# A two-layer graph network on one core: one-hot picks of source rows in place of a count matrix

## What is computed

```python
def _sage_layer(x, src, dst, deg_inv, Wl, bl, Wr):
    n = x.shape[0]
    agg = jax.ops.segment_sum(x[src], dst, num_segments=n) * deg_inv
    h = agg @ Wl.T + bl + x @ Wr.T
    norm = jnp.maximum(jnp.linalg.norm(h, axis=-1, keepdims=True), EPS)
    return jax.nn.relu(h / norm)

h = _sage_layer(x, src, dst, deg_inv, Wl0, bl0, Wr0)
h = _sage_layer(h, src, dst, deg_inv, Wl1, bl1, Wr1)
x = _layernorm(x + h)
```

## Time and profile before

| | |
|---|---|
| median of three runs | 7893.84 us (7893.78 to 7914.73) |
| profiled execution, span from first to last instruction | 8201.9 us |
| of it the edge stage with set-up | up to about 5,139 us |
| segment sum of layer 0 | 5,454 to 6,680 us |
| segment sum of layer 1 | 6,763 to 8,026 us, with node stages before and behind |
| one superblock in the profile | 86.6 to 87.7 us |

### The profile page before, as it was taken

One profiled execution on the slowest core, in us unless ns is written; L12 is line 12 of the kernel. 1 busy time (PEld: TensorE's weight loads), 2 busy tenths in 40 slices (PEclk: granted clock), 3 DMA queues, 4 the chain that ended last, 5 costly groups with the idle time before them and its releaser, 6 DMA issues. The chain is left out here.

```text
span 8201.9 us, 138821 instructions
## 1 busy us (share of the span) xinstructions
PE 7072.6 (86%) x39416; PEld 5215.0 (64%) x39416; DVE 4581.6 (56%) x16310; ACT 3033.9 (37%) x6076; POOL 5844.8 (71%) x4866
## 2 busy tenths in 40 slices
PE   5898988888998889989899999878888887888883
PEld 4777777777777777877788778543333353333332
DVE  5777777777777633333333333346666656666663
ACT  2222222222222222222222222356666666666664
POOL 5888888888778888888888887336666655666663
PEclk7777777777777766676666666679999978999995
DMA  4333333333333322222222222221111111111111
GB/s 125 33 35 35 34 34 34 34 35 34 34 34 34 33 27 27 27 27 27 27 28 27 28 27 26 82 54 20 20 20 20 21 42 34 21 21 20 20 21 50
DMA packets 652915, 273.41 MB, mean 33 GB/s; under 512 B 544598, under 2 KB 600314, under 8 KB 652360
## 3 DMA queue, kind: packets, MB, share of 16 engines
q0 software_dynamic: 325280, 163.91, 19.0%
q1 hardware_dynamic: 326500, 105.06, 5.9%
q10 hardware_dynamic: 900, 1.60, 0.1%
HBM read 189.59 MB, written 80.61 MB: 33 GB/s over the span
## 5 line engine op out<-in xcount | busy, mean ns | idle before, releaser
L653 POOL DMA_INDIRECT future<-sbuf,sidx x1564 | 2495.2, 1595 | 507.1 <-issue 457.8
L639 POOL DMA_INDIRECT gbuf<-in_x_dram,gidx x1564 | 1563.3, 1000 | 482.6 <-issue 471.1
L1441 ACT CAST dense<-bank 128x512 bf16<-128x512 f32 x2744 | 1572.9, 586 | 834.3 <-PE bank L1452 514.2
L1465 PE MATMUL bank<-dense,wide 128*128 128x512 bf16 x2744 | 1066.9, 389 | 248.2 <-ACT dense L1441 125.7
L1377 DVE TENSOR_SCALAR at_dst<-iota,metaf 128x512 bf16<-128x512 f16 x2758 | 919.0, 360 | 575.0 <-PE bank L1452 425.1
L1343 POOL DMA_INDIRECT gb<-x,nidx x728 | 781.3, 1073 | 495.6 <-DVE at_dst L1377 293.6
L1452 PE MATMUL bank<-at_dst,at_src 128*128 128x512 bf16 x2744 | 1057.0, 389 | 70.2 <-DVE at_dst L1377 70.2
L1343 POOL DMA_INDIRECT gb<-h,nidx x728 | 781.1, 1073 | 467.8 <-DVE at_dst L1377 271.8
L1466 PE MATMUL bank<-dense,wide 128*128 128x512 bf16 x2744 | 1062.8, 387 | 0.0
L965 PEld LDWEIGHTS bank<-w1pe,featT 96*128 96x128 f32 x3128 | 722.3, 269 | 305.8 <-issue 305.2
L966 PE MATMUL bank<-w1px,srcT 65*128 65x128 f32 x3128 | 815.5, 354 | 0.0
(11 more groups left out here) (255 smaller groups left out, 11505.8 us busy)
## 6 DMA issues: line engine op xcount, KB each, us to landing
gbuf<-in_x_dram,gidx POOLq DMA_INDIRECT x1564
comb<-in_edge_attr_dram SPq DMA_DIRECT2D x391, 64.0 KB
future<-sbuf,sidx POOLq DMA_INDIRECT x1564
blkb<-blkrow SPq DMA_DIRECT2D x210, 98.0 KB
future<-zero POOLq DMA_DIRECT2D x16, 800.0 KB, 17.7
fut<-future SPq DMA_DIRECT2D x100, 125.0 KB
gb<-x,nidx POOLq DMA_INDIRECT x732, 2.4
gb<-h,nidx POOLq DMA_INDIRECT x732, 2.5
```

What stands on the lines that cost most here:

```text
L639: pool.indirect_dma_start(out=gbuf[:, b, q, :], out_offset=None, in_=x[:, :], in_offset=bass.IndirectOffsetOnAxis(ap=gidx[:, b, q:q + 1], ...
L653: pool.indirect_dma_start(out=future[q][:, :], out_offset=bass.IndirectOffsetOnAxis(ap=sidx[:, b, q:q + 1], axis=0), in_=sbuf[:, b, q, :], ...
L1441: act.copy(dense[:, b % AR, :], psA[b % AR][:, :]).then_inc(t_cp, 1)
L1465: pe.matmul(psHM[:, :], pieces[:, b, 0:2 * D], dense[:, b % AR, :], start=(b == 0), stop=(b == BLOCKS - 1))
```

## The change

`adjacency` goes. In its place `rows_of` (PE) multiplies `at_src` by the block's `pieces` (192 columns: three pieces of 64) and so picks for each of the 128 slots the row of its source node, still as three exact bf16 pieces. Two steps make a pair: both picks write one bank of `psA` (192 columns each), and ACT copies both at once (2x192 columns) as bf16 into `rows16`. `apply` then uses the picked rows as weights and streams `at_dst` (not `dense`): two matmuls of 512 columns a step, as before. There are two banks of `psA`, two buffers of `rows16`, and two each of `psHM` and `psL`, used by turns of the superblock; the banks of `sums` go from three to two.

For the picks `at_src` has to be the other way round: source lanes on the partitions, slots along the row. The node stage before the layers turns the lane table of each superblock by a matmul with an identity (14), ACT copies them (4 copies), and one transfer stores them as `lanes`. In the layers SP loads seven rows of it at a time, broadcast to 128 partitions (`laneb`, 3 buffers, 196 loads of 128x896 f16 a layer), and `sources` becomes one TENSOR_SCALAR comparing that with the lane number.

`at_dst` has 14 buffers instead of 7; DVE makes it 8 steps ahead and, from step 14 on, waits for `apply` of 14 steps before instead of for `adjacency`. The sum of the three 64x512 results of a superblock moves to step 4 of the next one (`add_dense`); ACT moves the middle one in the third pair of the next.

```diff
-AR = 3
+AR = 2
+LEAD = 8
+DR = 14
+PW = XPCS * 64
...
             @block.scalar
             def _(act):
+                act.wait_ge(c_turned, 1)
+                for k in range(4):
+                    n = min(4, SBS - 4 * k)
+                    act.copy(lane16[:, 4 * k:4 * k + n, :],
+                             bank[1 + k][0:BLOCKS, 0:n * P].rearrange("b (s p) -> b s p", s=n)).then_inc(c_lane, 1)
+                act.wait_ge(c_lane, 4)
+                act.dma_start(lanes.rearrange("s b p -> b s p"), lane16[:, :, :]).then_inc(c_lane_st, 16)
...
             def _(pe):
+                for i in range(SBS):
+                    last = pe.matmul(bank[1 + i // 4][0:BLOCKS, (i % 4) * P:(i % 4 + 1) * P], meta[:, i, 0, :],
+                                     ident16[:, :], start=True, stop=True)
+                last.then_inc(c_turned, 1)
                 pe.wait_ge(c_ones, 1)
+                pe.wait_ge(c_lane, 4)
...
-SUM_SLOT = [0, 1, 2] * 4 + [1]
+SUM_SLOT = [0, 1] * 6 + [0]
...
                     def sources(k):
-
-                        dve.tensor_tensor(at_src[:, k % 2, :, :], iota16[:, 0:P].unsqueeze(1).to_broadcast([P, RING, P]),
-                                          metaf[:, 0, k * RING:(k + 1) * RING].unsqueeze(2).to_broadcast([P, RING, P]),
-                                          ALU.is_equal)
+                        dve.wait_ge(t_ln[k % 3], 16 * (k // 3 + 1))
+                        if k >= 2:
+                            dve.wait_ge(t_A, RING * (k - 1))
+                        dve.tensor_scalar(at_src[:, k % 2, :, :], laneb[:, k % 3, :, :], lane1[:, 0:1], None,
+                                          ALU.is_equal).then_inc(t_src, 1)
-                    def destinations(b):
-                        dve.tensor_scalar(at_dst[:, b % RING, :], iota16[:, :], metaf[:, 1, b:b + 1], None,
+                    def destinations(t):
+                        if t >= DR:
+                            dve.wait_ge(t_ap, t - DR + 1)
+                        b = t % BLOCKS
+                        dve.tensor_scalar(at_dst[:, t % DR, :], iota16[:, :], metaf[:, b:b + 1], None,
                                           ALU.is_equal).then_inc(t_at, 1)
...
-                    for i in range(SBS):
-                        for b in range(BLOCKS):
-                            act.wait_ge(t_A, BLOCKS * i + (b + 1))
-                            act.copy(dense[:, b % AR, :], psA[b % AR][:, :]).then_inc(t_cp, 1)
+                    for j in range(STEPS // 2):
+                        act.wait_ge(t_A, 2 * j + 2)
+                        act.copy(rows16[:, j % AR, :, 0:PW],
+                                 psA[j % AR][:, 0:2 * PW].rearrange("p (h k) -> p h k", h=2)).then_inc(t_cp, 1)
...
-                    def adjacency(i, b):
-                        pe.wait_ge(t_at, BLOCKS * i + (b + 1))
-                        pe.matmul(psA[b % AR][:, :], at_src[:, (b // RING) % 2, b % RING, :], at_dst[:, b % RING, :],
-                                  start=True, stop=True).then_inc(t_A, 1)
...
+                        if t % 2 == 0 and j >= AR:
+                            pe.wait_ge(t_cp, j - AR + 1)
+                        pe.matmul(psA[j % AR][:, (t % 2) * PW:(t % 2 + 1) * PW], at_src[:, (t // RING) % 2, t % RING, :],
+                                  pieces[:, b, :], start=True, stop=True).then_inc(t_A, 1)
...
+                        pe.wait_ge(t_at, t + 1)
+                        if b == 0 and i >= 2:
+                            pe.wait_ge(t_acc, ADDS * (i - 1) + ADDS - 1)
+                            pe.wait_ge(t_ms, i)
+                        pe.matmul(psHM[i % 2][:, :], rows16[:, j % AR, t % 2, 0:2 * D], at_dst[:, t % DR, :],
+                                  start=(b == 0), stop=(b == BLOCKS - 1))
+                        pe.matmul(psL[i % 2][:, :], rows16[:, j % AR, t % 2, 2 * D:4 * D], at_dst[:, t % DR, :],
                                   start=(b == 0), stop=(b == BLOCKS - 1)).then_inc(t_ap, 1)
```

More of the change, by code:

```diff
@@ L1019, in build @@
         mostrow = tmp("mostrow", [1, 4])
+        lane16 = tmp("lane16", [BLOCKS, SBS, P], F16)
         (c_left, c_mostT) = [tsem(f"c_left{i}") for i in range(2)]
+        (c_turned, c_lane, c_lane_st) = [tsem(f"c_lane{i}") for i in range(3)]
         (c_ones, c_s1, c_s2, c_sum, c_P, c_C, c_past, c_max, c_inv, c_I, c_flow, c_F, c_fT, c_H, c_hb, c_hc, c_O, c_yc,
@@ L1314, in build @@
             t_cp = lsem("cp")
-            t_end = lsem("end")
+            t_pad = lsem("pad")
+            t_src = lsem("src")
+            t_ln = [lsem(f"ln{b}") for b in range(3)]
             t_ap = lsem("ap")
@@ L1331, in _ @@
                         sp.dma_start(xf[:, c % 3, :, :], blocks_of[:, c * XB:(c + 1) * XB, :]).then_inc(t_xf[c % 3], 16)
+                        if c < 3:
+                            load_lanes(c)
+                    for k in range(3, CHUNKED):
+                        load_lanes(k)
                 @block.gpsimd
@@ L1475, in sums @@
                         for q in range(TILES):
-                            last = pe.matmul(psG[SUM_SLOT[m]][0:D, 0:W], gb1[:, m, q, :], oneh[:, ONE_SLOT[m], q, :],
+                            last = pe.matmul(psG(SUM_SLOT[m]), gb1[:, m, q, :], oneh[:, ONE_SLOT[m], q, :],
                                              start=(q == 0), stop=(q == TILES - 1))
                         last.then_inc(t_S, 1)
-                    for i in range(SBS):
-                        for b in range(BLOCKS):
-                            adjacency(i, b)
-                            if b >= 2:
-                                apply(i, b - 2)
-                            for m in range(POOLG):
-                                if b == TAKE[m]:
-                                    sums(i, m)
-                        apply(i, BLOCKS - 2)
-                        apply(i, BLOCKS - 1)
+                    for j in range(STEPS // 2 + 1):
+                        if j < STEPS // 2:
+                            rows_of(2 * j)
+                            rows_of(2 * j + 1)
+                        if j >= 1:
+                            for t in (2 * j - 2, 2 * j - 1):
+                                apply(t)
+                                for m in range(POOLG):
+                                    if t % BLOCKS == TAKE[m]:
+                                        sums(t // BLOCKS, m)
             clear(edge_sems)
@@ L1533, in _ @@
                             for q in range(TILES):
-                                last = pe.matmul(psG[0][0:D, 0:W], gb1[:, 0, q, :], oneh[:, 0, q, :],
+                                last = pe.matmul(psG(0), gb1[:, 0, q, :], oneh[:, 0, q, :],
                                                  start=(q == 0), stop=(q == TILES - 1))
```

109 lines of the change are left out of this document (69 added, 40 removed).

## The result

| | before | changed |
|---|---|---|
| median of 13 runs each | 7897.33 us | 7937.40 us |
| lowest, highest | 7892.24, 7914.73 | 7910.74, 7947.37 |
| ratio | | 1.0043, 95% interval 1.0036 to 1.0051 |
| profiled span | 8201.9 us | 7939.0 us |

The change makes the kernel slower, by 0.43%, where 7708 us and 2.4% faster were forecast, outside of the range of 7590 to 7880.

What follows compares the result with a forecast made beforehand. PE was taken to bound the segment sums before, POOL after: 28 x (76.3 - 69.4) = 193 us, less 2.4 + 4.8, gives 186 us saved, so 7893.8 - 186 = 7708 us; range 7590 to 7880.

Steps and rivals of the forecast that it cites:

- The time of a superblock before, 76.3 us from 87.3 less the 308 us: Segment sums before: profiled 87.3 us a superblock includes 11.0 us of late matmuls absent from timed runs, leaving 76.3.
- the rival that took the lateness for real, at 7445 us: Segment sums: late matmuls also occur when timed, so 87.3 us a superblock before and 71 after; 7445 us, chance 0.08.
- Span and median do come together: Changed kernel's profile: forecast a span some 300 us over the median; both coming together would show the late matmuls real.
- PE, 59.6 us: PE in the segment sums: 49 pairs of steps, 50.5 us, plus 9.1 for gathered groups make 59.6 us a superblock.
- the hidden hand-over: PE to ACT and back: picks and copy take about 0.8 us, hidden behind 1.03 us of PE work.
- the loads of lanes: SP's 196 loads a layer: one used each 4.9 us, three in flight, so they are hidden.
- The superblock's start: Start of each superblock: PE's 1.4 us wait while DVE empties the accumulators goes away.
- POOL is the bound: Segment sums after the change: POOL needs 65.4 us or more a superblock, against PE's 59.6 and DVE's 47.
- How long its gathers are: POOL's gathers: 4.0 us a superblock left over the bare floor of 65.4, where 6.4 stood, giving 69.4 us.
- I let these two cancel: POOL's gathers away from the superblock's start: at_src shrinking by 0.7 us offsets at_dst made in runs of about four.
- The rival "slower": POOL's gathers under DVE's runs of at_src and at_dst: mean gather over 1.16 us, about 8030 us; chance 0.11.
- The Trainium skill's rule: DVE and GpSimd share SBUF ports: the new at_src blocks GpSimd's descriptor writes, up to 5.0 us a superblock, about 7850.

Runs made afterwards that it cites:

- the second trace: The kernel before, unchanged, profiled once more: 7907.0 us in one execution, profiled span 7905.1 us.

## Why the prediction was wrong, point by point

- **The time of a superblock before, 76.3 us from 87.3 less the 308 us**: right in kind and 0.5 us high; the second trace has 75.8. That choice held, and the rival that took the lateness for real, at 7445 us, fell with it. Span and median do come together in the changed kernel, which I had named as a sign for that rival; the sign was badly chosen, since they also come together in the second trace of before.
- **PE, 59.6 us**: right, 59.6 measured without the gathers; picks 0.085 us apart, a pair 1.03. Its own 74.0 before measured 74.1.
- **ACT's copy 0.48 us, the hidden hand-over, at_src 0.36 us, the loads of lanes**: right. The copy has 479 ns, the new `at_src` stands 5741.97 - 5741.61 = 0.36 us ahead of the next instruction, and without the loads nothing is won.
- **The superblock's start**: right, PE's accumulators make it wait no more.
- **POOL is the bound**: right.
- **How long its gathers are**: this step failed. I had 6.4 us over the floor, took 1.9 off for the start, and wrote of the rest "I let these two cancel" and of "runs of about four". The runs became eight. DVE's limit of 14 buffers lets it start four steps at once behind a group, and in the time of those PE, with a step each 0.52 us against DVE's 0.26, frees the next ones; 4 / (1 - 0.26 / 0.52) = 8 `at_dst`, all that there are up to the next group, where I stopped counting at the first four. The term was 4.0 us over the floor of 65.4. Measured are 11.9, 65.36 + 11.86 = 77.2 in place of 69.4, and 28 x 7.8 = 218 us are most of the miss of 229. The kernel before had 52 x (1.060 - 0.952) = 5.6.
- **The loop**: I treated DVE's time as free, because it has 47 us of work in 69. But the idle time lies in 13 lumps, each of them a wait for the slower POOL, and each is followed by a run that slows POOL again. Less DVE work in total, more of it without a break.
- **The rival "slower"** had this mechanism, its place and its point of decision: it wanted a mean gather over 1.16 (1.15 with 75.8 us) and put 0.11 on it. The mean is 1.180. Its price, 8030 us, assumed a third of the gathers late by 0.9 us; it was a fifth, 301 of 1456, by 1.1 us ((1.180 - 0.952) x 1456 / 301). The argument against it, that DVE's total work falls, was the same mistake: the work did fall, from 707 to 544 us in the windows of 13 superblocks shown.
- **The Trainium skill's rule** ("SBUF — State Buffer", section "SBUF: two separate sides"): its direction was right and I gave it too little weight. Its price for `at_src`, up to 5.0 us a superblock, stands beside 52 x (1.180 - 1.102) = 4.1 us measured with an `at_src` of two elements. From its other half, that a two-input instruction of DVE collides only with a GpSimd instruction that reads SBUF, I took it that the old `at_src` did no harm. That was wrong: a gather reads its row numbers from `nidx`, which lies in SBUF, and both traces with a two-input `at_src` show gathers that end 0.82 to 0.84 us behind it (83 before, 158 in the changed kernel). That it is this reading that is held is my inference.

The difference adds up: 28 x (77.2 - 75.8) = 39 us, against 40 measured.

What stays open is what exactly lets a gather through. With breaks of 0.24 us most come through, with a float32 addition between sometimes. Of the 301 late ones of the changed kernel 96 end 0.12 to 0.14 us behind the end of a run of one-hots, and another 100 end 0.82 to 0.84 us behind one. The two add up to the bare 0.952, as if a gather could be held at one place close to its start and at one close to its end; that is a reading, and the other 105 fit neither.

## What to carry to other kernels

When an engine has slack, look at how its work lies in time and not only at its sum: a deeper buffer can turn waits into bursts, and a burst can hold up an engine that works on none of its data. Where POOL issues transfers of its own (indirect ones), keep DVE's one-hots paced and broken, and choose the number of buffers by the length of a gather. And a gain on one engine is worth only the distance to the next: here 14.5 us on PE against about 5, until the division of the work was moved after it.

## What the runs showed of the hardware

- A gather of 128 rows takes 0.952 us when DVE is quiet, and beside unbroken work of DVE, nearly all of it one-input 16-bit one-hots, up to 4.08 us in the changed kernel.
- A two-input 16-bit TENSOR_TENSOR of 1.09 us can hold a gather as well: of 220 late gathers that begin beside one, 158 end 0.82 to 0.84 us behind its end.
- 36 gathers of one and the same row in a superblock put the transfers' share at 0.79 where 0.32 stood beside, and made it 10 us longer; with other rows in their place it took 55.6 us in place of 68.8.
- One recorded execution of the kernel before had matmuls late by microseconds and 308 us in all; a second one of the same kernel had none. Where span and median differ so much, a second profile is worth having before the waits are read.
